# x loaded by row blocks between the blocks of adj, the first stores of the transposed matrix eight blocks late, and the identity turned at the start

## The reference

```
L0: u = p * (diag[:, None] * x @ W) + x      (rows below 2048 with W_u, diag_u, par_u; the others with W_i, diag_i, par_i)
    h = adj @ (adj.T @ u);  out = layernorm(h) * gamma + beta + x
L1: out = 1 - 0.1 * x - 0.01 * sum(x * (adj @ x), axis=1)
L2: out = unit rows of relu([x, (adj @ x + x) / deg] @ W + b),   deg = row sums of adj + 1
L3: three products with adj (a recurrence of degree 3), each times a 64 x 64 weight, summed
```

## Time and profile before

| | us |
|---|---|
| median of 3 runs | 1538.25 |
| their range | 1534.6 to 1538.72 |
| the profiled execution, its own time | 1534.9 |
| its span, first to last instruction | 1532.2 |
| PE busy | 1495.1 (98%) |
| DVE busy | 610.7 (40%) |
| ACT busy | 248.7 (16%) |

### The profile page before, as it was taken

How to read it: one execution, slowest core, us unless ns; L and a number is a source line. 1 busy time by engine, 2 the same in 40 slices (tenths; PEclk the granted TensorE clock), 3 DMA queues, 4 the chain that set the end, 5 groups by cost and what they waited for, 6 DMA issues and landing times.

```text
span 1532.2 us, 17411 instructions
## 1 busy us (share of the span) xinstructions
PE 1495.1 (98%) x6558; PEld 698.3 (46%) x6558; DVE 610.7 (40%) x1333; ACT 248.7 (16%) x492; POOL 61.3 (4%) x66
## 2 busy tenths in 40 slices
PE   7899999999999999999999899999999999999998
PEld 5555555554555543324444344443444444444332
DVE  4655656555565567524331444233111021010342
ACT  3334333343434310000100001000000000000000
POOL 0000000000000012100000011000000000000010
PEclk8999999999999999999999999999999999999999
DMA  9999999999999989999888488886388868988996
GB/s 313 408 388 407 411 404 392 387 396 392 382 398 389 360 324 389 420 421 410 295 313 296 176 320 289 296 299 250 114 329 315 305 227 342 339 312 299 370 419 255
DMA packets 122306, 519.09 MB, mean 339 GB/s; under 512 B 20940, under 2 KB 20980, under 8 KB 72180
## 3 DMA queue, kind: packets, MB, share of 16 engines
q1 hardware_dynamic: 105584, 412.68, 72.2%
q10 hardware_dynamic: 16644, 105.34, 16.5%
HBM read 411.82 MB, written 106.17 MB: 338 GB/s over the span
## 4 chain that ended last, share of the span: by engine, by line
issue 99%; POOLq 0%; POOL 0%; DVE 0%
POOL power_out L408 0%; POOLq L406 0%; POOLq L408 0%; DVE rows L872 0%; POOL ident L401 0%; POOLq L403 0%; POOL ident L403 0%; POOLq L1103 0%
## 5 line engine op out<-in xcount | busy, mean ns | idle before, releaser
L695 PE MATMUL ps_u<-blk,vectors 128*128 128x512 f32 (+1 forms) x2000 | 737.2, 596 | 1.1 <-DMA blk<-a_transposed 1.1
L695 PEld LDWEIGHTS ps_u<-blk,vectors 128*128 128x128 f32 (+1 forms) x2000 | 296.5, 173 | 394.7 <-issue 389.6
L454 ACT ACTIVATE blk<-ps_turn 128x512 f32<-128x512 f32 x400 | 203.4, 605 | 341.1 <-PE ps_turn L531 341.1
L1037 DVE TENSOR_TENSOR part<-part,ps_u 64x512 f32<-64x512 f32 (+1 forms) x45 | 30.8, 686 | 344.4 <-PE ps_u L695 343.7
L560 PE MATMUL ps_h<-blk,u_rows 128*64 128x512 f32 x720 | 164.4, 598 | 0.0
L793 DVE TENSOR_REDUCE row_part<-blk 128x4 f32<-128x2048 f32 x68 | 152.5, 2280 | 1.4 <-DMA blk<-in_adj 1.1
L531 PE MATMUL ps_turn<-ident,blk 128*128 128x128 f32 x1088 | 131.3, 280 | 10.5 <-DMA blk<-in_adj 10.5
L531 PEld LDWEIGHTS ps_turn<-ident,blk 128*128 128x128 f32 x1088 | 122.8, 145 | 30.9 <-issue 25.6
L777 DVE TENSOR_TENSOR part<-part,ps_h 128x512 f32<-128x512 f32 x80 | 55.0, 688 | 184.4 <-PE ps_h L560 184.4
L543 PE MATMUL ps_u<-blk,e 128*64 128x512 f32 x544 | 124.9, 599 | 0.0
L408 POOL TENSOR_TENSOR power_out<-power_in,minus_half 128x4 f32<-128x4 f32 x60 | 60.6, 1010 | 1467.3 <-DVEq L835 1467.3
(11 more groups left out here) (107 smaller groups left out, 557.2 us busy)
## 6 DMA issues: line engine op xcount, KB each, us to landing
blk<-a_transposed SPq DMA_DIRECT2D x291, 1024.0 KB, 5.4
a_transposed<-blk ACTq DMA_DIRECT2D x100, 1024.0 KB, 9.2
blk<-in_adj SPq DMA_DIRECT2D x68, 1024.0 KB, 13.4
nat_far<-in_adj SPq DMA_DIRECT2D x32, 1024.0 KB, 13.7
out<-rows SPq DMA_DIRECT2D x10, 128.0 KB, 4.2
rows<-in_x SPq DMA_DIRECT2D x1, 768.0 KB, 10.2
rows<-in_x SPq DMA_DIRECT2D x1, 512.0 KB, 7.3
w3x<-in_L_gnn_weight ACTq DMA_DIRECT2D x6, 16.0 KB, 7.9
```

The costliest lines, as they stand in the source:

```text
L454: nc.scalar.activation(blk[:, n % RING, t, :], ps_t[t][:, :], ACT.Copy)\
L695: mm = pe.matmul(acc, left, tiles[:, t, :], start=first, stop=last)
L1037: V.tensor_tensor(part[parts, cols], part[parts, cols], ps_both[r % 2][parts, :], ALU.add)\
```

## The change

SP now loads `x` in ten parts of 512 rows, part `i` directly ahead of block `i` of `adj`, each with a semaphore of its own. The loads of `par` and `w_i` move from SP's queue to ACT's, `par` ahead of all others there. PE transposes the identity 16 times before anything else, and turns the first rows of `x` ahead of block 0. The turned `diag` lands in `ps_u[0]` instead of `ps_u[1]`, and DVE computes `diag` after the first copy of `x`; it also sums block 0 before it makes row block 1 of `e`.

The stores lag. With `LATE = 8`, after odd block `n` of column `j` ACT has issued the stores of all blocks but the last `8 - j` (none behind from column 8 on). So column 0 issues two stores instead of ten, columns 1 to 8 eleven each, column 9 ten.

```diff
+    LATE = 8
+        diag_in = ps_u[0][:, 0:NT]
 (SP)
             for n in range(BLOCKS):
                 j, i = divmod(n, NB)
+                if j == 0:
+                    tiles = slice(i * TB, (i + 1) * TB)
+                    sp.dma_start(rows[:, tiles, :], x_rows[:, tiles, :]).then_inc(x_loaded[i], 16)
                 if n >= NAT:
                     ...
                 sp.dma_start(nat(n), a_blocks[...]).then_inc(nat_loaded[n % NAT], 16)
-                if n == 0:
-                    sp.dma_start(rows[:, 0:4 * TB, :], x_rows[:, 0:4 * TB, :]).then_inc(x_first_loaded, 16)
-                    sp.dma_start(par[:, 0, :], par_u.partition_broadcast(P)).then_inc(par_loaded, 16)
-                    sp.dma_start(par[:, 1, :], par_i.partition_broadcast(P)).then_inc(par_loaded, 16)
-                if n == 1:
-                    sp.dma_start(rows[:, 4 * TB:NT, :], x_rows[:, 4 * TB:NT, :]).then_inc(x_loaded, 16)
-                    for h in range(2):
-                        sp.dma_start(w0[half(h), 1, :], w_i).then_inc(x_loaded, 16)
 (ACT)
+            const(par[:, 0, :], par_u.partition_broadcast(P), par_loaded)
+            const(par[:, 1, :], par_i.partition_broadcast(P), par_loaded)
+            for h in range(2):
+                const(w0[half(h), 0, :], w_u)
             const(diag_flat[0:UT, :], ...)
             const(diag_flat[UT:NT, :], ...)
             for h in range(2):
-                const(w0[half(h), 0, :], w_u)
+                const(w0[half(h), 1, :], w_i, w_i_loaded)
...
+            def n_stored(n):
+                return max(0, n + 1 - max(0, LATE - n // NB))
...
                     if t == 0 and n % 2 == 1:
-                        store(n - 1)
-                if n % 2 == 1:
+                        for k in range(n_stored(n - 2), n_stored(n)):
+                            if k < n:
+                                store(k)
+                if n % 2 == 1 and n_stored(n) == n + 1:
                     store(n)
 (PE)
+            for k in range(16):
+                pe.transpose(ps_t[TB - 1][:, k % TB * P:(k % TB + 1) * P], ident[:, :], ident[:, :])
+            turn_x_in(0)
             turn_block(0)
             turn_diag()
-            turn_x_in(0)
+            times_w(0)
             turn_x_in(1)
-            times_w(0)
             turn_block(1)
 (DVE)
             copy_x_in(0)
+            dve.wait_ge(par_loaded, 32)
+            ... par_prod, then diag from diag_in (removed from ahead of copy_x_in(0))
             copy_x_in(1)
             make_e(0)
+            sum_rows(0)
             make_e(1)
```

More of the change, by code:

```diff
@@ L148, in build @@
         weights_loaded = sem("weights_loaded")
-        x_first_loaded = sem("x_first_loaded")
-        x_loaded = sem("x_loaded")
+        w_i_loaded = sem("w_i_loaded")
+        x_loaded = [sem(f"x_loaded{i}") for i in range(NB)]
         ident_ready = sem("ident_ready")
@@ L186, in build @@
         block = ctx.enter_context(nc.Block())
-        N_CONSTS, N_X_LOADS, N_WEIGHTS = 4, 3, 22
+        N_CONSTS, N_WEIGHTS = 4, 22
         N_ROOTS = 6 * NB
@@ L499, in turn_diag @@
                 pe.wait_ge(consts_loaded, 16 * N_CONSTS)
-                pe.matmul(ps_u[1][:, 0:NT], diag_flat[:, :], ident[0:NT, 0:NT], start=True, stop=True)\
+                pe.matmul(diag_in, diag_flat[:, :], ident[0:NT, 0:NT], start=True, stop=True)\
                     .then_inc(diag_turned, 1)
             def turn_x_in(i):
-                pe.wait_ge(x_first_loaded, 16)
-                if i > 3:
-                    pe.wait_ge(x_loaded, 16 * N_X_LOADS)
+                pe.wait_ge(x_loaded[i], 16)
                 if i > 1:
@@ L518, in times_w @@
                     pe.wait_ge(xw_used, i)
+                pe.wait_ge(w_i_loaded if i >= UB else consts_loaded, 32 if i >= UB else 16 * N_CONSTS)
                 for t in range(TB):
@@ L742, in _ @@
             V.tensor_tensor(ident2[:, :], ident[:, 0:F], ident[:, F:P], ALU.add)
[L743 to L749, removed]
             def by_pairs(t):
@@ L803, in _ @@
             copy_x_in(0)
+            dve.wait_ge(par_loaded, 32)
+            V.tensor_tensor(par_prod[:, :], par[:, :, 0], par[:, :, 1], ALU.mult)
+            dve.drain()
+            dve.wait_ge(diag_turned, 1)
+            V.tensor_scalar(diag[:, 0:UT], diag_in[:, 0:UT], par_prod[:, 0:1], None, ALU.mult)
+            V.tensor_scalar(diag[:, UT:NT], diag_in[:, UT:NT], par_prod[:, 1:2], None, ALU.mult)
+            dve.drain()
             copy_x_in(1)
             make_e(0)
+            sum_rows(0)
             make_e(1)
@@ L808, in _ @@
                 later = [i for i in (2 * p + 2, 2 * p + 3) if i < NB]
-                sum_rows(2 * p)
+                if p > 0:
+                    sum_rows(2 * p)
                 for i in later:
```

## The result

| | before | changed |
|---|---|---|
| median, us | 1538.25 (5 runs, 1534.6 to 1540.34) | 1527.04 (5 runs, 1526.59 to 1528.72) |
| the profiled execution, us | 1534.9 (span 1532.2) | 1526.59 (span 1524.7) |
| PE busy, us | 1495.1 | 1494.4 |

The ratio is 0.9933, with an interval from 0.9915 to 0.9952: some 10 us of 1538, between 7 and 13. The forecast was 1523.7 with a range from 1518 to 1531, faster. The sign, the place and the main mechanism hold; 12.9 us were forecast for column 0 and the profile shows 9.1. The profiled execution of before lies near the bottom of its five runs (1534.9 of 1534.6 to 1540.34), so the two profiles are 8.3 us apart and the medians 11.2.

What follows compares the result with a forecast made beforehand. Column 0 was taken as bound by DMA, the other nine by PE. Profiled 1534.9 us less 12.9 for column 0, nothing charged for returned stores, gave 1522.0; plus 1.7 towards the median, 1523.7, range 1518 to 1531.

Steps and rivals of the forecast that it cites:

- The rival in which the stores do not matter: Column 0 was set only by the first blocks' lateness; gain 5 us, time 1531; chance 0.05.
- Block 0 at 6.8 us: Start of column 0: block 0, loaded behind `x` part 0, lands at about 6.8 us.
- Block 0's transposes at the upper level: Start of column 0: after the burst, block 0's transposes take 1.97 us and end at 8.8 instead of 9.5.
- the rival on the clock: The clock stays or falls low at the start, costing 5.7 us in all, time 1529.4; chance 0.2.
- The 0.5 us for `diag`: Start of column 0: PE may stall for late constants before `turn_diag`, bounds 0 and 2.2 us; 0.5 taken.
- The wait for `make_e(1)` behind the sum: First pair: PE idles some 1.2 us before `turn_x_in(3)`; `x` part 3 bounds it, the sum's place costs only 0.3.
- The debt costs nothing: Columns 1 to 8: returned stores cost 7 us over PE's time at 402 GB/s, inside 10 absorbed; nothing charged.
- a sign that the prediction had named for the rival: PE waits for `blk<-in_adj` behind 100 us, if DMA bounds columns 1 to 8; chances 0.1 (1532.7 us) and 0.05 (slower).
- the 10 us that I let lateness absorb: Columns 1 to 8: loads landing after 22.7 us without a PE wait were taken to allow some 10 us.
- The signs: No store before 45 us, block 1 turned before 10.5, `u_turn_back` at 58.1, columns 53.9 apart, landings growing slowly from 13.
- ACT's wait for a ring place: Behind column 0: store 2's place is rewritten about 19 us after issue, its landing takes perhaps 14; no wait.
- From the profile to the median: Final sum: half of the 3.35 us between profiled execution and median, 1.7, is added to 1522.0, giving 1523.7.

Runs made afterwards that it cites:

- stores_only: The kernel before with the late stores alone, loads of `x` and start as before; 1527.44 us, ratio 0.9946 to before.
- start_only: The changed kernel with `LATE = 0`, so the stores go out as before; 1533.04 us, ratio 0.9980 to before.
- repaid_in_two: The changed kernel with the lag falling by four a column instead of one (8, 4, 0); 1541.22 us, ratio 1.0043 to before.
- par_row: The changed kernel with `par` loaded into one partition and spread over 128 by a matmul; 1525.98 us, ratio 0.9942 to before.
- shift: row_first_sum with the lag held at eight through column 1 and repaid in columns 2 to 9; 1522.48 us, ratio 0.9902 to before.
- row_and_first: par_row with block 0 also loaded ahead of the first two parts of `x`; 1524.74 us, ratio 0.9936 to before.
- row_first_sum: row_and_first with block 0's row sum behind `make_e(1)`, as before the change; 1523.36 us, ratio 0.9909 to before.
- shift_no_burst: shift without the 16 transposes of the identity; 1524.47 us, ratio 0.9918 to before.
- block_first_par: The changed kernel with block 0 ahead of `x` part 0, and `par` behind `diag` and `w_u` on ACT's queue; 1527.77 us, ratio 0.9941 to before.

## Why the prediction was right, and where it was off

- **Column 0 is bound by DMA, the others by PE: shown.** stores_only and start_only separate the stores from the start, and repaid_in_two shows that a column with 24 transfers is bound by DMA too. The rival in which the stores do not matter falls.
- **Pairs at 9.0 us and the last at 7.5: right.** 27.0 us for three pairs, and 7.1 for the last.
- **Block 0 at 6.8 us: the step that failed.** It was used at 9.27, 2.5 us late. The prediction let `par` "leave SP's queue" and counted the order of the queues, but not what `par` does to the DMA engines wherever it is issued. Its row was there: block 1, issued at 6.26, landed at 13.5, and the window of 8 to 9 us shows 0 GB/s. I had put that down to the blocked issue alone. par_row measured the term: 2.0 us on block 0. The other 0.5 us stay open.
- **Block 0's transposes at the upper level: wrong.** 3.68 in place of 1.97, 1.7 us. The burst was to be followed by a gap of 1 us; the gap was 3.6. A short gap alone would not have made it sure: in par_row (1.69 us) and in shift (0.86 us) block 0 ran at the low level too. The low level on block 0 is a part of the rival on the clock (1.3 of its 5.7 us), which I had given 0.2; the rest of it did not come, as block 1 ran at 1.91. These two terms are 4.2 us; the last pair gave 0.4 back, and 58.4 stands against 54.6.
- **The 0.5 us for `diag`: not spent.** PE goes on behind block 0 without a wait for it; block 0's lateness hid it. In row_and_first, with block 0 early, PE did wait 0.6 us for `diag_flat`.
- **The wait for `make_e(1)` behind the sum: right in place, wrong in its bound.** It was 1.64 us against 1.2. But `x` part 3, issued at 6.48, landed at 16.8, and PE asked for it at 17.4, so DVE alone held PE. `times_w(1)` ended at 17.0 and `make_e(1)` began at 18.36, so by an estimate from these rows the sum's place cost some 1.3 us at this point, not 0.3. That `x` part 3 is the bound is true of row_first_sum, where PE waits 0.96 us for it. So the first pair behind block 0's transposes came out within 0.1 us of the forecast partly by luck: the 0.5 for `diag` paid for the longer wait.
- **The debt costs nothing: nearly right in size, wrong in its reason.** 1.0 us came back, and a sign that the prediction had named for the rival did show, a wait of PE for a block behind 100 us (0.8 us at 136). The other kernels with all eight late have such a wait as well (1.9 us in stores_only, 1.4 in row_and_first); shift and shift_no_burst, which repay one column later, have none. The rate over 225 to 500 us is 411 GB/s and not 402, and the demand 22.02 MB in 53.74 us, 410. As the landings neither grow nor shrink there, and as repaid_in_two moves 411 while PE waits, the schedule runs just at the ceiling. But the 10 us that I let lateness absorb are not there: the landings were at 21 us in column 1 already, and in repaid_in_two PE waited once they had grown to 27 us and more. I had read 22.7 us without a wait as depth to spare, when it was nearly all of the depth. By an estimate from this, at a ceiling of 402 the eight columns would have lost most of their 7 us.
- **The signs.** No store ahead of 45 us (the first is at 53.72), no wait of PE for a DMA between 14 and 55 and columns 53.74 apart came as said. Block 1's transposes started at 14.50 instead of ending before 10.5, and `u_turn_back` of column 0 stands at 61.93 and not 58.1. The landings did not grow slowly from 13: they were at 15 us for issues of 55 to 80 and at 21 in the next window.
- **ACT's wait for a ring place: right, there was none** up to 545 us. Stores landed after 11.3 us at 72 to 125 us, inside the 19.
- **From the profile to the median: luck.** The profiled execution was forecast at 1522.0 and took 1526.59, 4.6 us more, 3.8 of them in column 0. The median came only 3.3 us over its forecast, since half of 3.35 us had been added by a guess and its profiled execution lies only 0.45 under the median. The changed kernel's runs lie in 2.1 us, those of before in 5.7. Part of the gain in the medians seems to be that the waits of column 0, which can throw the clock, are gone; no run tested that.

The HBM limit of about 358 GB/s per core that the Trainium skill gives (DMA: Bandwidth & Descriptors, section Specifications) does not hold here: with one core at work the trace has 411 over 275 us of loads and stores. The statement of the Trainium skill that transposes don't bring the clock up (TensorE: Matmul & The Clock Gate, Part 4: PE-mode transpose) does not hold either: in row_and_first PE did nothing but transposes before 7.9 us, and block 0's took 1.97.

## What to carry to other kernels

Where a phase is bound by transfers and the next one by compute, move the writes that nobody waits for into the next phase, but add up both loads and stores against the measured ceiling in each stretch, since a late landing is depth already spent. Look at the DMA rate microsecond by microsecond at the start: here two loads of 1 KB that gave every partition a few bytes held block 0 back by 2.0 us, though its whole megabyte takes only 2.6 us at 402 GB/s; load such values into one partition and spread them by a matmul. Don't count on a burst to bring the clock up: here it showed an effect only where the first block followed within about 1 us, and not in every profile.

## What was not expected of the hardware

- While two loads of 1 KB, each 8 bytes to 128 partitions, were under way on ACT's queue, the DMA engines moved 113 to 161 GB/s for 3 us in the changed kernel and 164 to 191 in block_first_par, where the rate is above 300 once `par` has landed. In the kernel before, with the two on SP's own queue, the rate was 0 from 8 to 9 us and 41 from 9 to 10, though block 1 had been issued at 6.26. Why is open.
- The granted clock reads 1.00 from the start of the span, though block 0's transposes at 9.27 us took the low level's 3.68 us; up to its first change in the records only the pace tells the level.
- The same burst and a gap of 0.86 to 1.14 us behind it left block 0 at the upper level in three profiles (1.97 us: block_first_par, row_and_first, row_first_sum) and at the low one in one (3.68 us, shift).
